# Biases on diagonals minus weights: a set-up step moved to GpSimd, and a new order of the beginning and the end

## The chip, the cores and the metric

The kernel runs on one core of a Trainium2 chip. The metric is the device time of one execution in microseconds (us). A core has five engines with their own instruction queues: TensorE (PE; its weight loads are shown as PEld), VectorE (DVE), ScalarE (ACT), GpSimd (POOL) and SyncE (SP), which here only issues transfers. They meet through semaphores: an instruction waits for a count, and later instructions of the same queue wait behind it.

## The reference

The input x has 32 sequences of 256 tokens with 128 channels. The reference is one layer of a transformer, cut here to what is computed:

```
n  = layernorm(x)                                  # over the 128 channels
Q, K, V = n W_Q + b_Q, n W_K + b_K, n W_V + b_V    # 16 heads of 64
A  = softmax(Q K^T / 8)
y  = concat(A V) W_O + b_O
x1 = x + layernorm(y)
m  = layernorm(x1)
z  = m W + (1/16) sum_e softmax(m G)_e * V_e U_e m   # 8 experts of rank 16
out = x1 + layernorm(z)
```

All of it is in float32. For every query, key and weight of the attention the kernel keeps a high part and a low part (`_hi`, `_lo`), and it forms the products of high with high, high with low and low with high.

## The kernel before

A sequence is worked on in eight pairs of heads. For each pair TensorE projects queries and keys (`project_qk`, lines 434 to 436, into the bank `qk_ps`). ScalarE takes the high part, VectorE or GpSimd the low part (`qk_lo`). TensorE forms the scores (`scores`, line 468, into one of two banks `st_ps`), VectorE finds the row maxima (`row_max`, line 1317), ScalarE the exponentials (line 860), VectorE the inverse sums and GpSimd scales the probabilities (`scale_probs`, line 1805). VectorE transposes them in blocks (`transpose_blocks`), SyncE moves the blocks of four pairs with 16 transfers (`move_blocks`, line 313), and TensorE multiplies with the values (`probs_v`, line 493). Then come the output projection (line 527), the layer norms and the experts. Several sequences are in flight: the scores of sequence i, the probabilities times values of i - 1 and i - 2, and the rest of i - 3 or i - 4.

The order of the work is written out by hand for each engine: a beginning (sequences 0 to 3), a loop whose body stands once per sequence (4 to 30), and an end (31 and what is left of 28 to 30). The loop is the same before and after the change.

The set-up is done once in the beginning. The layer norm before the projections has a constant of 1 added to every channel instead of the bias (line 841, `xt_high`), so each query and key weight needs a correction: bias minus column mean of the weights. `weight_means` makes it on TensorE in six pieces. The first two pieces are the 256 early columns of the query and of the key weights, the other four are 384 late columns each. For a piece, one product of a matrix of -1/128 with the weights (line 379) gives minus the mean, and for each pair of heads one product of a broadcast bias column with the identity over 128 (line 383) adds the bias. VectorE adds the result to the weights (`fold_means`, line 1223); ScalarE and VectorE then split the weights in a high and a low part (`weight_hi`, line 834, and `weight_lo`, line 1214). `value_sums` (line 392) sums the value weights with 8 products of one column each. GpSimd centres the output weights (`centre_w_o`, line 1763), and VectorE centres the rows of the experts' weights (`centre_ffn_rows`, lines 1283 to 1290).

## Time and profile before

| | |
|---|---|
| time, median of 3 runs (lowest to highest) | 978.57 us (977.16 to 979.06) |
| the profiled execution's own time | 978.71 us |
| its span between first and last instruction | 976.9 us |
| granted TensorE clock, mean over the span | 0.998 of full speed |
| busy: PE / PEld | 963.7 us (99%) / 777.3 us (80%) |
| busy: DVE / ACT / POOL | 909.9 us (93%) / 887.9 us (91%) / 759.9 us (78%) |

The span starts with the first instruction on any engine. The time has 1.8 us more than the span, which lie around it. A matmul in float32 is recorded as two instructions, so a product that stands once in the program can be counted twice in the trace.

### The profile page before, as it was taken

Reading aid. Unit: us, or ns where it says so; the run is one execution under the profiler, and the core shown is the slowest. Engines: PE = TensorE matmul, PEld = TensorE weight load, DVE = VectorE, ACT = ScalarE, POOL = GpSimd, SP = SyncE. Lnnn points to the kernel's source line nnn. Section 1 sums busy time; section 2 is a strip of 40 time slices with the busy share of each in tenths; the row PEclk is TensorE's granted clock in tenths of the full one; section 3 lists DMA queues with packets and bytes.
Section 4 is the critical chain, followed back from the end, with each engine's and each line's share of the span. In section 5 each row is a group of like instructions: output and inputs, shape, how many; then the busy total and the mean of one; then the engine's idle time right before and its main releaser. Section 6 shows DMA issues by size and latency. Waiting matters only on the chain.

```text
span 976.9 us, 28184 instructions
## 1 busy us (share of the span) xinstructions
PE 963.7 (99%) x8628; PEld 777.3 (80%) x8628; DVE 909.9 (93%) x1666; ACT 887.9 (91%) x3183; POOL 759.9 (78%) x746
## 2 busy tenths in 40 slices
PE   8999999999999999999999999999999999999997
PEld 7768888778888878888878888877888877878875
DVE  5999999999999999999999999999999999999972
ACT  4999999999999999999999999999999999999872
POOL 2777988888888788878878878887888878877862
PEclk9999999999999999999999999999999999999999
DMA  7276775666676665676666676566677666667560
GB/s 267 55 164 138 171 164 134 141 151 137 158 172 139 137 153 137 148 177 144 138 151 138 137 177 155 137 149 141 138 166 164 138 138 152 138 156 167 131 157 12
DMA packets 58467, 143.32 MB, mean 147 GB/s; under 512 B 16960, under 2 KB 25664, under 8 KB 58432
## 3 DMA queue, kind: packets, MB, share of 16 engines
q1 hardware_dynamic: 58432, 142.89, 63.4%
q8 instruction: 18, 0.29, 0.1%
q14 instruction: 17, 0.14, 0.0%
HBM read 6.50 MB, written 4.19 MB: 11 GB/s over the span
## 4 chain that ended last, share of the span: by engine, by line
PE 93%; SPq 2%; DVE 2%; ACT 1%; issue 1%; DMA 0%; POOL 0%; POOLq 0%; DVEq 0%; ACTq 0%
PE o_ps L493 24%; PE st_ps L468 21%; PE extra_ps L527 9%; PE qk_ps L434 6%; PE qk_ps L435 6%; PE qk_ps L436 6%; PE xv_ps L448 4%; PE extra_ps L358 3%; PE xv_ps L450 3%; PE xv_ps L449 3%; PE extra_ps L549 2%; SPq L313 2%; PE extra_ps L562 2%; PE extra_ps L564 1%; PE xv_ps L358 1%
## 5 line engine op out<-in xcount | busy, mean ns | idle before, releaser
L1805 POOL TENSOR_TENSOR probs<-probs,inv_sum 128x1024 f32<-128x1024 f32 x256 | 484.4, 1896 | 115.6 <-DVE inv_sum L1325 108.4
L860 ACT ACTIVATE probs<-st_ps,neg_max 128x256 f32<-128x256 f32 x1024 | 476.8, 496 | 33.6 <-DVE neg_max L1317 31.8
L1317 DVE TENSOR_REDUCE neg_max<-st_ps 128x4 f32<-128x1024 f32 x256 | 308.3, 1205 | 12.6 <-PE st_ps L468 11.7
L1336 DVE STREAM_TRANSPOSE probs_b<-probs 128x1024 f32<-128x1024 f32 x252 | 309.0, 1229 | 1.1 <-POOL probs L1805 1.1
L493 PE MATMUL o_ps<-probs_t,v_sb 128*64 128x256 f32 x2048 | 249.3, 385 | 1.6 <-DMA probs_t<-probs_b 0.9
L860 ACT ACTIVATION_READ_ACCUMULATOR probs<-st_ps,neg_max 128x1 f32 x1024 | 231.5, 226 | 0.0
L493 PEld LDWEIGHTS o_ps<-probs_t,v_sb 128*64 128x64 f32 x2048 | 135.9, 136 | 81.1 <-DVE o_lo L1351 10.4
L468 PE MATMUL st_ps<-qk_hi 64*128 64x256 f32 x1024 | 162.8, 314 | 1.3 <-ACT probs L860 0.8
L846 ACT CAST qk_hi<-qk_ps 128x512 fp32r<-128x512 f32 x256 | 153.2, 598 | 11.9 <-PE qk_ps L436 7.0
L468 PE MATMUL st_ps<-qk_lo,qk_hi 64*128 64x256 f32 x1024 | 145.4, 279 | 0.0
L468 PE MATMUL st_ps<-qk_hi,qk_lo 64*128 64x256 f32 x1024 | 144.8, 278 | 0.0
L1312 DVE TENSOR_TENSOR qk_lo<-qk_ps,qk_hi 128x512 fp32r<-128x512 f32 x192 | 130.3, 678 | 6.2 <-ACT qk_hi L846 2.4
L468 PEld LDWEIGHTS st_ps<-qk_hi 64*128 64x128 f32 x1024 | 97.1, 186 | 28.0 <-issue 7.2
L1351 DVE TENSOR_TENSOR o_lo<-o_ps,o_hi 128x512 fp32r<-128x512 f32 x128 | 87.7, 685 | 13.7 <-ACT o_hi L875 10.0
L468 PEld LDWEIGHTS st_ps<-qk_lo,qk_hi 64*128 64x128 f32 x1024 | 98.0, 187 | 0.0
L468 PEld LDWEIGHTS st_ps<-qk_hi,qk_lo 64*128 64x128 f32 x1024 | 98.0, 187 | 0.0
L1778 POOL TENSOR_TENSOR rstd<-var_eps,neg_half 128x2 f32<-128x2 f32 x128 | 88.9, 694 | 10.0
L875 ACT CAST o_hi<-o_ps 128x512 fp32r<-128x512 f32 x128 | 80.2, 627 | 7.1 <-PE o_ps L493 7.0
L434 PE MATMUL qk_ps<-xt_hi,wq_hi 128*128 128x256 f32 x256 | 84.4, 330 | 1.3 <-DVE qk_lo L1312 0.6
L1799 POOL TENSOR_TENSOR qk_lo<-qk_full,qk_hi 128x512 fp32r<-128x512 f32 x64 | 82.2, 1284 | 3.6 <-ACT qk_full L853 2.0
L882 ACT COPY v_sb<-xv_ps 128x512 f32<-128x512 f32 x128 | 77.2, 603 | 0.3 <-PE xv_ps L450 0.3
L527 PE MATMUL extra_ps<-o_hi,wo_hi 128*128 128x256 f32 x256 | 72.6, 284 | 0.0
(140 smaller groups left out, 1952.6 us busy)
## 6 DMA issues: line engine op xcount, KB each, us to landing
probs_t<-probs_b SPq DMA_DIRECT2D x1008, 128.0 KB, 2.3
out<-x_all SPq DMA_DIRECT2D x31, 128.0 KB, 1.9
x_all<-in_x SPq DMA_DIRECT2D x1, 3840.0 KB, 17.4
probs_b<-in_w_v SPq DMA_DIRECT2D x1, 512.0 KB, 4.5
probs_b<-in_w_o SPq DMA_DIRECT2D x1, 512.0 KB, 6.3
probs_b<-in_w_q SPq DMA_DIRECT2D x1, 384.0 KB, 4.8
probs_b<-in_w_k SPq DMA_DIRECT2D x1, 384.0 KB, 5.4
x_all<-in_x SPq DMA_DIRECT2D x2, 128.0 KB, 3.2
```

Source lines behind the costliest of these rows:

```text
L434: nc.tensor.matmul(dst, w_hi[w][:, cols], xt_hi[turn][:, :], start=True, stop=False)
L468: last = nc.tensor.matmul(st_ps[p % 2][:, (2 * h + j) * T:(2 * h + j + 1) * T], tile(q, j)[head_rows(h), :], k[head_rows(h), :], start=(t ...
L493: last = nc.tensor.matmul(o_ps[head_rows(h), cols], v_sb[turn][:, s, p * P + h * DH:p * P + (h + 1) * DH], probs_t[chunk % 2][:, :, s, fir ...
L527: last = nc.tensor.matmul(extra_ps[:, 0:T], w["o"][:, cols], o[:, pair, :], start=(pair == pairs[0] and n == 0), stop=(pair == pairs[-1] a ...
L846: nc.scalar.copy(qk_hi_sb[p % N_QK][:, :], qk_ps[:, :]).then_inc(qk_hi_ready, 1)
L860: last = nc.scalar.activation(probs[n][:, h, j, :], st_ps[p % 2][:, (2 * h + j) * T:(2 * h + j + 1) * T], ACT.Exp, bias=neg_max[n][:, h, j ...
L1312: nc.vector.tensor_tensor(qk_lo_sb[n][:, :], qk_ps[:, :], f32(qk_hi_sb[n][:, :]), ALU.subtract).then_inc(qk_lo_ready, 1)
L1317: nc.vector.tensor_reduce(neg_max[p % N_PROBS][:, :, :].rearrange("p h j -> p (h j)"), st_ps[p % 2][:, :].rearrange("p (j s) -> p j s", j= ...
L1336: nc.vector.transpose(probs_b[chunk % 2][:, :, :, 2 * NT * n:2 * NT * (n + 1), :].rearrange("p i t n q -> p n t i q"), probs[p % N_PROBS][ ...
L1351: nc.vector.tensor_tensor(o_lo[:, pairs, :].rearrange("p g q -> p (g q)"), o_ps[:, :], f32(o_hi[:, pairs, :]).rearrange("p g q -> p (g q)" ...
L1778: nc.gpsimd.tensor_tensor(rstd[ln][:, :], var_eps[ln][:, :], neg_half[:, :], ALU.pow).then_inc(rstd_ready[ln], 1)
L1805: nc.gpsimd.tensor_tensor(probs[n][:, :, :, :].rearrange("p h j s -> p (h j) s"), probs[n][:, :, :, :].rearrange("p h j s -> p (h j) s"), ...
```

## The change

For the four late pieces the two kinds of products become one. GpSimd makes, for queries and for keys, a tensor of 128 by 768 (`less`): it puts the biases on the diagonals of six 128 by 128 blocks (`bias_on_diagonal`) and, when the late weights have landed, subtracts them (`less_weights`). The column mean of that tensor is bias over 128 minus the mean weight on every row, which one product with a matrix of 1/128 gives (`mean_w`). The two early pieces stay as they were. The tensors `less` lie in the buffer into which the first blocks of probabilities are moved later, so the first `move_blocks` waits for the sixth piece.

The hand-written order of the beginning and of the end changes on all engines. The core of the diff, with the functions in full and of the orders the places that matter below:

```diff
+        less = {n: probs_t[0][:, i, :, :, :].rearrange("p t n q -> p (t n q)")[:, 0:(PAIRS - 2) * P] for i, n in enumerate("qk")}
...
             def move_blocks(b, chunk):
                 transposed = PAIRS * b + (chunk + 1) * CHUNK
+                if first(b) and chunk == 0:
+                    sp.wait_ge(mean_projected, len(MEANS))
...
             def weight_means(piece):
 
                 n, cols, bank = MEANS[piece]
...
+                else:
+                    if piece >= 3:
+                        pe.wait_ge(mean_folded, piece)
+                    pe.wait_ge(less_ready[n], 1)
+                    last = nc.tensor.matmul(bank[:, 0:cols.stop - cols.start], mean_w[:, :],
+                                            less[n][:, cols.start - 2 * P:cols.stop - 2 * P], start=True, stop=True)
                 last.then_inc(mean_projected, 1)
...
             weight_means(1)
+            value_sums()
+            weight_means(2)
             transpose_xn(0)
-            weight_means(2)
+            weight_means(3)
             project_qk(0, 0, 0)
-            weight_means(3)
+            weight_means(4)
             project_v(0, 0, 0, free=(xt_lo_ready, 1))
-            weight_means(4)
+            weight_means(5)
             project_qk(0, 1, 0)
-            weight_means(5)
             scores(0, 0)
-            value_sums()
+            project_v(0, 1, 0, free=(v_copied[0], 1))
             project_qk(0, 2, 0)
...
+            store(29)
             move_blocks(31, 0)
-            store(29)
...
+            def bias_on_diagonal(n):
+
+                pool.wait_ge(bias_loaded, 16)
+                pool.wait_ge(constants_ready, 1)
+                column = (B_Q if n == "q" else B_K) + 2
+                nc.gpsimd.tensor_tensor(per_pair(less[n]), ident[:, :].unsqueeze(1).to_broadcast([P, PAIRS - 2, P]),
+                                        bias[:, column:column + PAIRS - 2].unsqueeze(2).to_broadcast([P, PAIRS - 2, P]),
+                                        ALU.mult).then_inc(diagonal_ready[n], 1)
+
+            def less_weights(n):
+                pool.wait_ge(diagonal_ready[n], 1)
+                pool.wait_ge(w_loaded[n], 16)
+                nc.gpsimd.tensor_tensor(less[n], less[n], stage[n][:, late],
+                                        ALU.subtract).then_inc(less_ready[n], 1)
...
+            bias_on_diagonal("q")
+            bias_on_diagonal("k")
             ln_rstd(LN_X, 1)
-            centre_w_o()
+            less_weights("q")
+            less_weights("k")
             ln_rstd(LN_X, 2)
             qk_lo(0, 1)
+            centre_w_o()
             scale_probs(0, 0)
```

In the queue of GpSimd the beginning of the set-up stood like this before (`probs_b` is where the loaded weights are staged, `var_eps` and `rstd` belong to the layer norms, `qk_lo` to the first pair that GpSimd splits):

```order
L1828 AFFINE_SELECT ident<-ident 128x128
L1771 TENSOR_TENSOR var_eps<-mean_var,eps 128x2
L1778 TENSOR_TENSOR rstd<-var_eps,neg_half 128x2
L1763 TENSOR_TENSOR probs_b<-probs_b,w_o_mean 128x1024
L1771 TENSOR_TENSOR var_eps<-mean_var,eps 128x2
L1778 TENSOR_TENSOR rstd<-var_eps,neg_half 128x2
L1799 TENSOR_TENSOR qk_lo<-qk_full,qk_hi 128x512
L1805 TENSOR_TENSOR probs<-probs,inv_sum 128x1024
```

The same place on GpSimd now (`probs_t` is the buffer in which `less` lies):

```order
L1854 AFFINE_SELECT ident<-ident 128x128
L1784 TENSOR_TENSOR probs_t<-ident,bias 128x768 x2
L1797 TENSOR_TENSOR var_eps<-mean_var,eps 128x2
L1804 TENSOR_TENSOR rstd<-var_eps,neg_half 128x2
L1791 TENSOR_TENSOR probs_t<-probs_t,probs_b 128x768 x2
L1797 TENSOR_TENSOR var_eps<-mean_var,eps 128x2
L1804 TENSOR_TENSOR rstd<-var_eps,neg_half 128x2
L1825 TENSOR_TENSOR qk_lo<-qk_full,qk_hi 128x512
L1771 TENSOR_TENSOR probs_b<-probs_b,w_o_mean 128x1024
L1831 TENSOR_TENSOR probs<-probs,inv_sum 128x1024
```

Four operations of 768 columns are new, two of them behind the first `rstd`, and the centring of the output weights has gone behind the first `qk_lo`.

In the queue of VectorE the set-up went on after the two early folds like this before (`xt_lo` is the low part of the transposed input, `wv_lo` and the like are low parts of weights, folds are the additions of `o_ps`):

```order
L1214 SCALAR_TENSOR_TENSOR wq_lo<-probs_b,wq_hi 128x256
L1214 SCALAR_TENSOR_TENSOR wk_lo<-probs_b,wk_hi 128x256
L1266 SCALAR_TENSOR_TENSOR xt_lo<-xv_ps,xt_hi 128x256
L1223 TENSOR_TENSOR probs_b<-probs_b,o_ps 128x384
L1214 SCALAR_TENSOR_TENSOR wv_lo<-probs_b,wv_hi 128x1024
L1312 TENSOR_TENSOR qk_lo<-qk_ps,qk_hi 128x512
L1223 TENSOR_TENSOR probs_b<-probs_b,o_ps 128x384
L1272 TENSOR_REDUCE w_o_mean<-probs_b 128x8
L1275 TENSOR_SCALAR w_o_mean<-w_o_mean 128x8
L1223 TENSOR_TENSOR probs_b<-probs_b,o_ps 128x384
L1283 TENSOR_REDUCE ffn_mean<-ffn 128x1 x2
L1286 TENSOR_SCALAR ffn_mean<-ffn_mean 128x2
```

The same place on VectorE now, from the normalisation of the first x on:

```order
L1258 TENSOR_SCALAR xn<-x_all,mean_var,rstd 128x128 x2
L1233 TENSOR_TENSOR probs_b<-probs_b,st_ps 128x256
L1224 SCALAR_TENSOR_TENSOR wv_lo<-probs_b,wv_hi 128x1024
L1224 SCALAR_TENSOR_TENSOR wk_lo<-probs_b,wk_hi 128x256
L1250 BN_AGGR mean_var<-stats 128x2 x2
L1233 TENSOR_TENSOR probs_b<-probs_b,o_ps 128x384
L1224 SCALAR_TENSOR_TENSOR wq_lo<-probs_b,wq_hi 128x256
L1276 SCALAR_TENSOR_TENSOR xt_lo<-xv_ps,xt_hi 128x256
L1233 TENSOR_TENSOR probs_b<-probs_b,o_ps 128x384
L1282 TENSOR_REDUCE w_o_mean<-probs_b 128x8
L1285 TENSOR_SCALAR w_o_mean<-w_o_mean 128x8
L1233 TENSOR_TENSOR probs_b<-probs_b,o_ps 128x384
```

The low part of the value weights and the first late fold now stand ahead of `xt_lo`, for which the first projection waits, and the rows of the experts' weights are no longer centred here.

They are centred on VectorE during the scores of sequence 1, where these rows stand now:

```order
L1322 TENSOR_TENSOR qk_lo<-qk_ps,qk_hi 128x512
L1293 TENSOR_REDUCE ffn_mean<-ffn 128x1 x2
L1296 TENSOR_SCALAR ffn_mean<-ffn_mean 128x2
L1300 TENSOR_SCALAR ffn<-ffn,ffn_mean 128x128 x2
L1335 RECIPROCAL inv_sum<-row_sum 128x4
```

Nothing of the experts stood between the low parts and the inverse sums of that place before.

## Rows read from the trace of the kernel before

**Rows 1.** Windows: start:end, us, busy us of each engine, clock, DMA share, GB/s

```profile
core 0: us, PE busy (x) PEld busy (x) DVE busy (x) ACT busy (x) POOL busy (x), PEclk, DMA share, GB/s
30.00:40.00 10.00, 9.87 (x84) 8.22 (x84) 9.68 (x18) 9.41 (x32) 8.35 (x8) 1.00 0.01 3
40.00:50.00 10.00, 8.55 (x74) 6.61 (x72) 9.82 (x15) 10.00 (x38) 9.26 (x7) 1.00 0.70 157
60.00:70.00 10.00, 10.00 (x88) 7.15 (x89) 9.31 (x15) 8.55 (x28) 6.53 (x7) 1.00 0.62 141
950.00:960.00 10.00, 8.59 (x71) 5.72 (x69) 4.15 (x14) 4.26 (x16) 2.37 (x6) 1.00 0.23 55
```

**Rows 2.** Timeline of TensorE in the set-up: start, us, engine, line, what [idle before]

```profile
11.05 0.36 PE L434 MATMUL qk_ps<-xt_hi,wq_hi 128*128 128x256 f32 x1 [0.34 <-DVE xt_lo L1266]
...
12.49 0.83 PE L383 MATMUL o_ps<-probs_t,bias 128*128 128x128 f32 x6
13.07 0.48 PE L448 MATMUL xv_ps<-wv_hi,xt_hi 128*128 128x512 f32 x1
...
18.61 1.95 PE L392 MATMUL st_ps<-one,probs_b 128*128 128x1 f32 x16
20.41 0.36 PE L434 MATMUL qk_ps<-xt_hi,wq_hi 128*128 128x256 f32 x1
```

**Rows 3.** Timeline of SyncE's queue: the issue of the late query weights

```profile
3.54 0.43 SPq L297 DMA_DIRECT2D probs_b<-in_w_q  x1
```

**Rows 4.** DMA issues: KB each, us from issue to landing

```profile
probs_b<-in_w_q SPq DMA_DIRECT2D x1, 384.0 KB, 4.8
```

**Rows 5.** Timeline of GpSimd in the set-up

```profile
15.32 1.90 POOL L1763 TENSOR_TENSOR probs_b<-probs_b,w_o_mean 128x1024 f32<-128x1024 f32 x1 [10.46 <-DVE w_o_mean L1275]
...
19.79 1.58 POOL L1799 TENSOR_TENSOR qk_lo<-qk_full,qk_hi 128x512 fp32r<-128x512 f32 x1 [1.64 <-ACT qk_hi L846]
27.59 1.89 POOL L1805 TENSOR_TENSOR probs<-probs,inv_sum 128x1024 f32<-128x1024 f32 x1 [6.22 <-DVE inv_sum L1325]
```

**Rows 6.** Line 1799 over the whole span: ns min/median/max, first and last start

```profile
L1799 POOL TENSOR_TENSOR qk_lo<-qk_full,qk_hi x64: 1272/1279/1579, 19.8 to 926.8; 128x512 fp32r<-128x512 f32 x64
```

**Rows 7.** Timeline of VectorE in the set-up

```profile
15.07 0.17 DVE L1275 TENSOR_SCALAR w_o_mean<-w_o_mean 128x8 f32<-128x8 f32 x1
...
16.05 0.47 DVE L1283 TENSOR_REDUCE ffn_mean<-ffn 128x1 f32<-128x128 f32 x2
16.56 0.69 DVE L1286 TENSOR_SCALAR ffn_mean<-ffn_mean 128x2 f32<-128x2 f32 x1
17.28 0.48 DVE L1290 TENSOR_SCALAR ffn<-ffn,ffn_mean 128x128 f32<-128x128 f32 x2
...
19.27 0.96 DVE L1214 SCALAR_TENSOR_TENSOR wk_lo<-probs_b,wk_hi 128x768 fp32r<-128x768 f32 x1
20.15 1.22 DVE L1317 TENSOR_REDUCE neg_max<-st_ps 128x4 f32<-128x1024 f32 x1
...
22.22 0.69 DVE L1312 TENSOR_TENSOR qk_lo<-qk_ps,qk_hi 128x512 fp32r<-128x512 f32 x1 [0.78 <-ACT qk_hi L846]
24.47 1.23 DVE L1317 TENSOR_REDUCE neg_max<-st_ps 128x4 f32<-128x1024 f32 x1 [1.55 <-PE st_ps L468]
25.61 1.22 DVE L1214 SCALAR_TENSOR_TENSOR wo_lo<-probs_b,wo_hi 128x1024 fp32r<-128x1024 f32 x1
```

**Rows 8.** Windows, as rows 1, behind the value sums

```profile
23.00:24.00 1.00, 1.00 (x10) 1.00 (x12) 0.00 (x0) 1.00 (x7) 0.00 (x0) 0.50 0.00 0
```

**Rows 9.** Timeline of the end, TensorE, GpSimd and SyncE

```profile
935.01 1.95 PE L493 MATMUL o_ps<-probs_t,v_sb 128*64 128x256 f32 x16 [0.91 <-DMA probs_t<-probs_b]
...
959.90 0.38 PE L527 MATMUL extra_ps<-o_hi,wo_hi 128*128 128x256 f32 x1
...
943.27 0.75 POOL L1816 TENSOR_TENSOR x_all<-z,x 128x256 f32<-128x256 f32 x1
...
940.69 10.10 SPq L313 DMA_DIRECT2D probs_t<-probs_b  x16
```

More of the change, by code:

```diff
@@ L327, in _ @@
             move_blocks(2, 1)
+            move_blocks(3, 0)
             store(0)
-            move_blocks(3, 0)
             move_blocks(3, 1)
@@ L615, in _ @@
             project_qk(1, 0, 1)
-            project_v(1, 1, 1, free=(v_copied[0], 2))
             scores(0, 6)
@@ L647, in _ @@
             project_qk(2, 2, 0)
+            project_v(2, 1, 0, free=(v_copied[0], 3))
             ffn_means()
@@ L653, in _ @@
             project_qk(2, 3, 0)
-            project_v(2, 2, 0, free=(v_copied[1], 3))
             output_projection(0)
@@ L670, in _ @@
             scores(2, 5)
+            transpose_xn(3, free=(v_copied[3], 3))
             project_qk(2, 7, 0)
-            project_v(3, 0, 1, free=(xt_lo_ready, 4))
             scores(2, 6)
             project_tg(0, free=(x1t_ready, 1))
+            project_v(3, 0, 1, free=(xt_lo_ready, 4))
             project_qk(3, 0, 1)
+            scores(2, 7)
             project_v(3, 1, 1, free=(v_copied[0], 4))
+            project_qk(3, 1, 1)
             probs_v(1, 4, 1)
             probs_v(1, 5, 1)
-            project_qk(3, 1, 1)
-            scores(2, 7)
             scores(3, 0)
@@ L685, in _ @@
             probs_v(1, 7, 1)
+            scores(3, 1)
             project_z(0, free=(ut_ready, 1))
@@ L688, in _ @@
             project_v(3, 2, 1, free=(v_copied[1], 4))
-            scores(3, 1)
             scores(3, 2)
+            project_v(3, 3, 1, free=(v_copied[2], 4))
             project_qk(3, 4, 1)
-            project_v(3, 3, 1, free=(v_copied[2], 4))
             output_projection(1, free=(z_copied, 1))
@@ L940, in _ @@
             weight_hi("v", every, w_hi_ready)
+            weight_hi("k", early, early_hi_ready, 2)
             weight_hi("q", early, early_hi_ready, 1)
-            weight_hi("k", early, early_hi_ready, 2)
             xt_high(0, 0)
+            weight_hi("q", late, w_hi_ready, 4)
             qk_hi(0, 0)
-            weight_hi("q", late, w_hi_ready, 4)
             copy_v(0, 0, 0)
-            qk_full(0, 1)
-            weight_hi("o", every, w_hi_ready)
             weight_hi("k", late, w_hi_ready, 6)
             qk_hi(0, 1)
+            qk_full(0, 1)
+            copy_v(0, 1, 0)
             qk_hi(0, 2)
+            exponentials(0, 0, 1)
             exponentials(0, 0, 0)
-            exponentials(0, 0, 1)
-            copy_v(0, 1, 0)
+            copy_v(0, 2, 0)
             qk_hi(0, 3)
+            exponentials(0, 1, 0)
             exponentials(0, 1, 1)
-            exponentials(0, 1, 0)
-            copy_v(0, 2, 0)
             qk_hi(0, 4)
+            exponentials(0, 2, 1)
             exponentials(0, 2, 0)
-            exponentials(0, 2, 1)
             copy_v(0, 3, 0)
@@ L965, in _ @@
             exponentials(0, 3, 0)
+            xt_high(1, 1)
             qk_hi(0, 6)
             exponentials(0, 3, 1)
-            xt_high(1, 1)
-            exponentials(0, 4, 1)
+            weight_hi("o", every, w_hi_ready)
             qk_hi(0, 7)
             exponentials(0, 4, 0)
+            exponentials(0, 4, 1)
             copy_v(1, 0, 1)
@@ L1183, in _ @@
-            copy_last(4)
             exponentials(31, 7, 1)
@@ L1414, in _ @@
             spread_x(1)
+            fold_means(0)
             norm_first_x()
+            fold_means(1)
+            weight_lo("v", every, w_hi_ready, w_lo_ready)
             spread_landed(LN_X, 1)
-            settle()
+            weight_lo("k", early, early_hi_ready, early_lo_ready)
             aggregate_x(1)
-            fold_means(0)
-            fold_means(1)
+            fold_means(2)
             weight_lo("q", early, early_hi_ready, early_lo_ready)
-            weight_lo("k", early, early_hi_ready, early_lo_ready)
             xt_low(0, 0)
-            fold_means(2)
-            weight_lo("v", every, w_hi_ready, w_lo_ready)
-            qk_lo(0, 0)
             fold_means(3)
@@ L1429, in _ @@
             fold_means(4)
-            centre_ffn_rows()
+            qk_lo(0, 0)
+            offset_values()
             fold_means(5)
@@ L1842, in _ @@
             scale_probs(0, 4)
+            qk_lo(1, 1)
             scale_probs(0, 5)
-            norm_x(2)
-            qk_lo(1, 1)
             scale_probs(0, 6)
@@ L1927, in _ @@
             ln_rstd(LN_Y, 30)
+            ln_rstd(LN_X1, 30)
+            qk_lo(31, 5)
             scale_probs(31, 1)
-            qk_lo(31, 5)
-            ln_rstd(LN_X1, 30)
             scale_probs(31, 2)
```

531 lines of the change are left out of this document (267 added, 264 removed).

## The prediction

> **What bounds the kernel now.** I read the windows first, to see which stretches leave TensorE idle. From 60 to 70 us TensorE is busy without a gap [rows 1], and so it stays through the loop, which the change leaves alone: there TensorE is the bound. The beginning is different. Between 30 and 50 us VectorE is busy 9.68 and 9.82 of 10 us and ScalarE 9.41 and 10.00, while TensorE misses 1.45 us of the second ten [rows 1]. Until about 55 us the chain through row maxima and exponentials sets the pace, and a microsecond counts there only if VectorE's list gets shorter or starts earlier. The end has gaps again, 1.41 us from 950 to 960 [rows 1]. Then I read the timelines of the set-up, to see who waits for whom, and that of the end. A gain in the beginning reaches the end whole if it still stands when TensorE becomes the bound.
>
> **The four products.** A late piece's six recorded bias products stand from 12.49 to 13.07 us, 0.58 us [rows 2]. Four pieces free 4 x 0.58 = 2.3 us of TensorE. In the loop that would be 2.3 us of the time. Here TensorE runs ahead of VectorE, so I cost it at nothing by itself; the second rival below lives on it.
>
> **The value sums.** They take 18.61 to 20.41, 1.80 us [rows 2], and move ahead of the third piece. There TensorE will wait for VectorE anyway (below), which hides them. At the old place they leave room, but VectorE's weight work lasts to 20.15 [rows 7], so their going gains at most 0.26 us by itself.
>
> **The new work on GpSimd.** The trace has no such operation of 768 columns. From below it is bounded by 1.28 us for 512 [rows 6], from above by 1.90 us for 1024 [rows 5]. I take 1.5 us for each diagonal and, as two full tensors are read, 1.8 us for each subtraction. The diagonals lie in an empty stretch: GpSimd idles 10.46 us before 15.32 [rows 5]. The first `rstd` is queued behind them and comes about 3 us later; the normalisation that waits for it now stands behind a fold on VectorE, so that this is hidden too. The subtraction for q starts when the late query weights have landed, at 3.54 + 4.8 = 8.34 us [rows 3, 4], and the one for k would end at about 12.0 if nothing interfered. TensorE's third piece waits for the first of them, and behind it in TensorE's queue stand the transposes of the first x and every projection. The first `move_blocks` waits for the sixth piece, which is made long before the first blocks are; it costs nothing.
>
> **What interferes.** Two places show VectorE and GpSimd holding each other up. GpSimd's low part takes 1.272 to 1.279 us at the least and in the median of 64 cases, but 1.579 in one [rows 6]: the first, at 19.79, while VectorE's `wk_lo` of 19.27, which reads two tensors from SBUF, still ran [rows 5, 7]. The 0.30 us are about what was left of that operation. The other way round, the scaling of `ffn_mean` (2 columns) took 0.69 us where its sister of 8 columns took 0.17 [rows 7]: it started at 16.56 and ended at 17.25, when GpSimd's centring of 15.32 had ended at 17.22 [rows 5]. So a VectorE operation with two inputs in SBUF, or a scaling from SBUF to SBUF, does not run beside a GpSimd operation that reads SBUF. After the change such pairs meet: from 8.34 to about 12 us VectorE wants to normalise the first x and to make `wv_lo` and `wk_lo`.
>
> The Trainium skill ("SBUF — State Buffer", section "Who interferes with whom") has this as a rule that speaks against the change: the two engines share one pair of ports, held for a whole instruction, by a VectorE operation with two SBUF inputs or in a two-port mode. By that rule the new work costs waits on both engines; without it the sum would be that of the first rival. The trace agrees in the two places just named.
>
> So I lay the work end to end: 8.34, two subtractions (3.6), `wv_lo` (1.2, as `wo_lo`), `wk_lo` and `wq_lo` of the early columns (at most 0.45 each, as 768 columns take 0.96) [rows 7], one fold (0.5, a 384-wide operation, by half of the same row), and `xt_lo` with an aggregation (0.5, an estimate from the same row). That is 15.0. If VectorE gets some turns between the subtractions it is 14.3, if it loses all of them 15.8. The first projection, at 11.05 now [rows 2], then starts at 15.0.
>
> From there to the first row maximum VectorE has three more folds (1.5), the means of the output weights (1.2, a reduction as wide as a row maximum's 1.22, and 0.17), a `qk_lo` (0.6), the value offset (0.15) and the two late low parts (1.9) [rows 7]: 5.5 us. The row maximum stands at 20.5 against 20.15 now: **+0.35**.
>
> **After the first row maximum.** Now VectorE waits 0.78 and then 1.55 us [rows 7]. The second wait is for scores that TensorE made late and slowly: the granted clock was 0.50 from 23 to 24 [rows 8], the lower level of 1.2 GHz, after the value sums, which moved single columns. With the value sums done early the two waits may go: 0 to -2.3, and I take **-2.3**, since the second quarter of the values is projected ahead of time as well. The centring of the experts' rows comes into this full stretch: 0.47 + 0.69 + 0.48 = 1.64 as it stood, 1.12 without its own wait [rows 7]; between them **+1.4**. The low part `wo_lo` moves from 25.61, where GpSimd was in 6.22 us of idle time [rows 5, 7], to a place beside scalings of 1.89 us [rows 5]: it waits 0 to 1.9. Since the next inverse sum stands behind it on VectorE, at most one scaling runs then; I take **+0.5**. The beginning: 0.35 - 2.33 + 1.4 + 0.5 = -0.1 us.
>
> **The end.** The work is the same in another order. TensorE waits 0.91 us at 935.01 for blocks of sequence 30 [rows 9]. VectorE's new order finishes the last of these transposes some 1.2 us earlier (a row maximum of 1.22 us [rows 7] moves behind it), but TensorE comes earlier too, since project_qk(31, 7) and scores(31, 6) now stand behind. I walked on with the durations of before and find the last output projection 0.5 us earlier than 959.90 [rows 9]: **-0.5**. The bounds are -2.3, if the 0.91 and 1.41 us of gaps close, and +1.5, if as much opens. What follows it is unchanged. On SyncE store(29) stands ahead of the last sixteen transfers; GpSimd has its data one scaling earlier than now, so I cost it at nothing (the last rival is its price).
>
> **Sum.** -0.1 - 0.5 = -0.6 us on the profiled execution's own 978.71 us gives 978.1; that execution lies 0.14 above the median, so 978.0 against 978.57. About 0.2% (2.0 us) is what a measurement of this kernel can tell from no change. The forecast is no change that can be told, with an own range of 976.6 to 979.8.
>
> **Rivals.**
> *No mutual wait (chance 0.27).* If the normalisation and the low parts run beside the subtractions, the first projection needs q's subtraction (10.15), one product (0.7), a fold, `wq_lo` and `xt_lo` (1.5) and some 0.7 of hand-overs: 13.0 instead of 15.0, and `wo_lo` costs nothing. That is 2.5 us better than the forecast: 975.5. For it: in the loop the two engines run side by side all the time. Against it: the rows of 1.58 and 0.69 us.
> *All of TensorE's saving arrives (0.05).* The 2.3 us of products and VectorE's 2.3 us of waits both come off: 974.0. Against it: 9.82 of 10 us on VectorE.
> *Slower: GpSimd wins every turn (0.18).* It takes k's subtraction directly behind q's, and later a scaling ahead of `wo_lo`. The first projection starts at 15.8 (0.8 more); TensorE stands idle for some 3 us right behind the value sums, its clock falls as before 23 us, and a piece's products take twice their 0.58 (0.6 more); `wo_lo` waits all its 1.9 (1.4 more). That is 2.8 us worse: 980.8. It decides from a first projection behind 15.8.
> *Slower: the store holds the last blocks (0.05).* The sixteen transfers start at 940.69 now, and the data of store(29) was ready at 943.27 + 0.75 = 944.0 [rows 9]. If it comes no earlier, they start up to 3.3 us later; half of that as the price gives 979.7.
> The forecast has 0.45. Faster by over 0.2% are the first two, 0.32; slower the last two, 0.23. The range of 975.2 to 980.6 reaches into both sides and leaves out their far ends, about 0.2 together.
>
> **What would show it.** In the profile after: two GpSimd operations of about 1.8 us from 8.3 us on; the normalisation of x, `wv_lo` or `wk_lo` lasting far longer than its width explains; the first projection near 15.0 and the first row maximum near 20.5 us; a long `wo_lo`; the last output projection 0.6 us earlier than 959.9. A first projection near 13 us beside short low parts would prove the first rival. TensorE idle between 60 and 70 us, where it has no gap now, would break the whole sum.

## The result and the profile after

The changed kernel takes 982.63 us in the median of 8 runs (980.67 to 985.34), the kernel before 978.62 in 8 runs beside it. The ratio is 1.0043, with its 95% interval in brackets [1.0032, 1.0054]: 4.0 us slower by the medians, and above the range of the prediction (975.2 to 980.6). The profiled execution took 983.44 us, 0.8 above the median, with a span of 981.66 against 976.92.

Three landmarks split the 4.74 us between the two spans: the first row maximum on VectorE, the 16th output projection on TensorE (in the unchanged loop), and the end of the span.

| | first projection | first row maximum | from there to the 16th output projection | from there to the end |
|---|---|---|---|---|
| before | 11.05 | 20.15 | 493.34 | 463.43 |
| after | 15.19 | 23.11 | 494.01 | 464.54 |
| difference | +4.14 | +2.96 | +0.67 | +1.11 |

So most of the loss is made before the first row maximum. The windows of the changed kernel (start, length, busy us of each engine, granted clock, DMA share, GB/s), the last four of which answer to [rows 1]:

```profile
10.00:20.00 10.00, 7.31 (x23) 5.11 (x23) 8.01 (x13) 2.00 (x5) 4.55 (x4) 0.67 1.07 381
30.00:40.00 10.00, 9.57 (x77) 8.16 (x75) 9.85 (x15) 9.39 (x32) 8.17 (x7) 0.87 0.01 2
40.00:50.00 10.00, 8.84 (x73) 7.12 (x73) 9.14 (x13) 9.03 (x31) 7.16 (x4) 0.96 0.61 136
60.00:70.00 10.00, 9.78 (x89) 6.95 (x85) 10.00 (x17) 8.98 (x32) 5.48 (x5) 1.00 0.57 128
950.00:960.00 10.00, 8.50 (x70) 6.01 (x72) 5.66 (x21) 4.50 (x17) 3.80 (x6) 1.00 0.60 136
```

The first line is the one to look at: from 10 to 20 us TensorE is busy 7.31 of 10 us, and its granted clock is 0.67 in the mean, so it ran for a large part at the lower level of 1.2 GHz. GpSimd's timeline (start, duration, instruction, in brackets the idle time before it) shows the new work, where [rows 5] had nothing:

```profile
3.14 2.89 POOL L1784 TENSOR_TENSOR probs_t<-ident,bias 128x768 f32<-128x768 f32 x2 [0.89 <-DMA bias<-in_biases]
8.73 4.66 POOL L1791 TENSOR_TENSOR probs_t<-probs_t,probs_b 128x768 f32<-128x768 f32 x2 [1.75 <-DMA probs_b<-in_w_q]
23.30 1.29 POOL L1825 TENSOR_TENSOR qk_lo<-qk_full,qk_hi 128x512 fp32r<-128x512 f32 x1 [8.15 <-ACT qk_full L863]
```

The two subtractions (L1791) fill 8.73 to 13.39 us. VectorE beside them, and on to the first row maximum [rows 7]:

```profile
8.89 0.41 DVE L1233 TENSOR_TENSOR probs_b<-probs_b,st_ps 128x256 f32<-128x256 f32 x1
9.22 2.50 DVE L1224 SCALAR_TENSOR_TENSOR wv_lo<-probs_b,wv_hi 128x1024 fp32r<-128x1024 f32 x1
11.65 2.02 DVE L1224 SCALAR_TENSOR_TENSOR wk_lo<-probs_b,wk_hi 128x256 fp32r<-128x256 f32 x1
...
13.75 0.52 DVE L1233 TENSOR_TENSOR probs_b<-probs_b,o_ps 128x384 f32<-128x384 f32 x1
...
16.00 0.56 DVE L1233 TENSOR_TENSOR probs_b<-probs_b,o_ps 128x384 f32<-128x384 f32 x1 [1.07 <-PE o_ps L394]
...
18.57 0.56 DVE L1233 TENSOR_TENSOR probs_b<-probs_b,o_ps 128x384 f32<-128x384 f32 x1 [0.67 <-PE o_ps L394]
...
20.77 0.55 DVE L1233 TENSOR_TENSOR probs_b<-probs_b,o_ps 128x384 f32<-128x384 f32 x1 [0.98 <-PE o_ps L394]
...
23.11 1.22 DVE L1327 TENSOR_REDUCE neg_max<-st_ps 128x4 f32<-128x1024 f32 x1
```

Two things are to be seen. The low parts are stretched: `wv_lo` lasts 2.50 us where `wo_lo`, as wide, took 1.22 [rows 7], and a `wk_lo` of 256 columns lasts 2.02 us, more than one of 768 columns (0.96 in [rows 7]). Because of the two the third fold comes at 13.75, though its weight mean was done at 11.6. Then each later fold waits for TensorE, 1.07 + 0.67 + 0.98 = 2.72 us. And TensorE [rows 2]:

```profile
8.65 1.84 PE L402 MATMUL st_ps<-one,probs_b 128*128 128x1 f32 x16
10.70 0.91 PE L394 MATMUL o_ps<-probs_t,mean_w 128*128 128x384 f32 x2 [0.20 <-POOL probs_t L1791]
11.45 0.38 PE L363 MATMUL xv_ps<-ident,xn 128*128 128x128 f32 x2
14.32 1.65 PE L394 MATMUL o_ps<-probs_t,mean_w 128*128 128x384 f32 x2 [2.49 <-DVE probs_b L1233]
15.19 0.99 PE L444 MATMUL qk_ps<-xt_hi,wq_hi 128*128 128x256 f32 x1
```

It stood idle for 2.49 us until the third fold was done. A weight mean (L394) of the same size took 0.91 us ahead of the gap and 1.65 behind it; the granted clock is 0.50 from 13.4 to 20.2 us, as windows of 1 us show:

```profile
12.00:13.00 1.00, 0.00 (x0) 0.00 (x0) 1.00 (x1) 0.34 (x1) 1.00 (x1) 1.00 1.09 387
14.00:15.00 1.00, 0.68 (x1) 0.50 (x2) 0.93 (x3) 0.00 (x0) 0.92 (x2) 0.50 1.09 387
19.00:20.00 1.00, 1.00 (x3) 0.75 (x3) 0.79 (x3) 0.15 (x1) 0.00 (x0) 0.50 1.09 389
21.00:22.00 1.00, 1.00 (x14) 0.86 (x14) 1.00 (x2) 0.64 (x1) 0.00 (x0) 1.00 0.03 11
```

At the end the chain of waits (start, us, what) runs through SyncE's queue [rows 9]:

```profile
929.14 0.59 SPq L318
929.77 1.72 SPq L318
931.53 0.59 SPq L318
...
935.34 2.48 DMA probs_t<-probs_b
937.87 1.95 PE o_ps L503 x16
```

SyncE issues one transfer behind the other here, each in 0.59 us; one took 1.72, and TensorE waited 1.16 us for the last of them:

```profile
937.87 0.87 PE L503 MATMUL o_ps<-probs_t,v_sb 128*64 128x256 f32 x6 [1.16 <-DMA probs_t<-probs_b]
```

### The profile page after: what moved, and what is told of

Its sections match the earlier page's. It is cut to its first block, busy times and chain, and to the rows that moved or that the text cites. A ratio compares the mean times of both kernels' runs of the same rounds, so it can differ in the third digit from the quotient of the medians.

```text
span 981.7 us, 28141 instructions
## 1 busy us (share of the span) xinstructions
PE 963.9 (98%) x8604; PEld 776.4 (79%) x8604; DVE 912.6 (93%) x1664; ACT 887.8 (90%) x3183; POOL 767.0 (78%) x750
## 4 chain that ended last, share of the span: by engine, by line
PE 90%; DVE 3%; SPq 2%; ACT 2%; issue 1%; DMA 1%; POOL 0%; POOLq 0%; DVEq 0%; ACTq 0%
PE o_ps L503 23%; PE st_ps L478 20%; PE extra_ps L537 9%; PE qk_ps L444 6%; PE qk_ps L446 6%; PE qk_ps L445 6%; PE xv_ps L458 4%; PE extra_ps L363 3%; PE xv_ps L460 3%; PE xv_ps L459 3%; SPq L318 2%; PE extra_ps L559 2%; PE extra_ps L572 2%; PE extra_ps L574 1%; ACT probs L870 1%
## 5 line engine op out<-in xcount | busy, mean ns | idle before, releaser
L1327 DVE TENSOR_REDUCE neg_max<-st_ps 128x4 f32<-128x1024 f32 x256 | 307.9, 1204 | 12.8 <-PE st_ps L478 11.6
L870 ACT ACTIVATION_READ_ACCUMULATOR probs<-st_ps,neg_max 128x1 f32 x1024 | 228.5, 223 | 0.0
L1361 DVE TENSOR_TENSOR o_lo<-o_ps,o_hi 128x512 fp32r<-128x512 f32 x128 | 87.7, 685 | 13.4 <-ACT o_hi L885 10.0
L444 PE MATMUL qk_ps<-xt_hi,wk_hi 128*128 128x256 f32 x256 | 72.6, 284 | 0.0
```

Source lines behind the costliest of these rows:

```text
L444: nc.tensor.matmul(dst, w_hi[w][:, cols], xt_hi[turn][:, :], start=True, stop=False)
L870: last = nc.scalar.activation(probs[n][:, h, j, :], st_ps[p % 2][:, (2 * h + j) * T:(2 * h + j + 1) * T], ACT.Exp, bias=neg_max[n][:, h, j ...
L1327: nc.vector.tensor_reduce(neg_max[p % N_PROBS][:, :, :].rearrange("p h j -> p (h j)"), st_ps[p % 2][:, :].rearrange("p (j s) -> p j s", j= ...
L1361: nc.vector.tensor_tensor(o_lo[:, pairs, :].rearrange("p g q -> p (g q)"), o_ps[:, :], f32(o_hi[:, pairs, :]).rearrange("p g q -> p (g q)" ...
```

## The experiments

Each experiment was timed beside the kernel before, whose medians there were 978.46 to 978.82 us; each ratio is taken to it. The interval of a ratio is 0.9 to 1.7 us to either side, so a difference between the medians of two experiments is uncertain by 1.3 us or more. The landmarks come from one profiled execution of each kernel. In the expectations a remainder is a low part.

**First split: end, beginning, products, clock.** Experiment 1 has only the new end:

```diff
             store(28)
+            store(29)
             move_blocks(31, 0)
-            store(29)
```

and the same for the other engines' lists behind the loop.

> The kernel before with the new order of the last blocks alone (all five engines from block 30 on). In the two traces the steady stretch of the changed kernel lies 3.65 us later and its end 1.08 us later again. Theory A (two separate losses, the set-up 3.65 and the end 1.1): 978.6 + 1.1 = 979.7 us, first output projection at 74.7 as before, last one at 961.0. Rival B (the end is neutral and lost its microsecond only because it was entered in another state): 978.6 us within 0.3.

Measured: 978.88 us, ratio 1.000 [0.9991, 1.0010]. By itself the new end neither costs nor gives anything that can be told; theory A's sum of two separate losses fails here, and rival B holds. Experiment 2 is the rest of the change without those hunks.

> The changed kernel with the old order of the last blocks: GpSimd's work and the new order of the beginning alone. Theory A: 978.6 + 3.65 = 982.2 us, TensorE idle 2.5 us before the fourth weight mean, granted clock near 0.67 between 10 and 20 us, first output projection at 77.6, last one at 963.5. Rival B: the whole loss sits here, 982.6 us or more, and the old end gives nothing back.

Measured: 980.87 us, ratio 1.0029 [1.0019, 1.0039]. That is below both expectations. Half of the loss or more sits in the beginning, and the new beginning is 1.8 us better by the medians with the old end than with the new one; the two intervals still overlap. Its profiled execution met the weights' landing 1 us later, `wv_lo` escaped (1.22 us), `wk_lo` did not (2.02). Experiment 3 keeps the new orders and takes GpSimd's work away:

```diff
-            bias_on_diagonal("q")
-            bias_on_diagonal("k")
-            less_weights("q")
-            less_weights("k")
```

with `weight_means` of the kernel before.

> The changed kernel in its new orders, but the four late weight means are made as before (one mean product and three bias products each, straight from the loaded weights), and GpSimd makes no diagonals and subtracts nothing. Theory A (VectorE and GpSimd hold each other up, TensorE stands idle behind them and its clock falls): wv_lo and the early wk_lo back to 1.22 and 0.42 us, no idle of 2.5 us, no clock fall between 13 and 20 us, first row max at 20 to 20.5 in place of 23.1, first output projection at 74 to 75.5, and 979 to 980 us, the rest being the end's 1.1. Rival C (the new order itself is at fault: value sums and the value remainder put ahead of the folds): first row max still at 22 or later and 981.5 us or more.

Measured: 980.45 us, 1.0015 [1.0005, 1.0024], between the two theories. VectorE's remainders are short again and the clock is 1.00 from 10 to 20 us, yet the first projection stands at 14.80 and the first row maximum at 21.88 (this execution, of 981.55 us, was the slowest of the 11):

```profile
9.55 1.84 PE L397 MATMUL st_ps<-one,probs_b 128*128 128x1 f32 x16
11.25 0.89 PE L384 MATMUL o_ps<-probs_b,probs_t 128*128 128x384 f32 x2
...
13.46 0.91 PE L384 MATMUL o_ps<-probs_b,probs_t 128*128 128x384 f32 x2 [0.43 <-DVE probs_b L1228]
14.21 0.83 PE L388 MATMUL o_ps<-probs_t,bias 128*128 128x128 f32 x6
14.80 0.37 PE L439 MATMUL qk_ps<-xt_hi,wq_hi 128*128 128x256 f32 x1
```

VectorE's folds wait for TensorE here:

```profile
12.85 0.56 DVE L1228 TENSOR_TENSOR probs_b<-probs_b,o_ps 128x384 f32<-128x384 f32 x1 [1.05 <-PE o_ps L388]
15.08 0.56 DVE L1228 TENSOR_TENSOR probs_b<-probs_b,o_ps 128x384 f32<-128x384 f32 x1 [1.00 <-PE o_ps L388]
...
17.31 0.56 DVE L1228 TENSOR_TENSOR probs_b<-probs_b,o_ps 128x384 f32<-128x384 f32 x1 [0.34 <-PE o_ps L388]
...
19.54 0.55 DVE L1228 TENSOR_TENSOR probs_b<-probs_b,o_ps 128x384 f32<-128x384 f32 x1 [1.00 <-PE o_ps L388]
...
21.88 1.22 DVE L1322 TENSOR_REDUCE neg_max<-st_ps 128x4 f32<-128x1024 f32 x1
```

So the new order with the old products is slower than before as well: value sums and two whole weight means stand ahead of the first projection, and TensorE is the chain. Experiment 4 was to hold the clock:

```diff
             transpose_xn(0)
+            warm_up(5)
             weight_means(3)
```

> The changed kernel with five more throw-away products (0.46 us each, as in its warm-up) behind the first transposes, where TensorE stood idle 2.5 us. VectorE's and GpSimd's work is untouched. Theory A1 (the fall of the clock after that idle costs most of the loss at the first row max): clock 1.0 through 10 to 20 us, the fourth weight mean 0.9 us long in place of 1.65, VectorE's three waits for folds down from 2.7 to below 1 us in sum, first row max at 21.0 to 21.5, and 980.5 us. Rival A2 (VectorE's lengthened remainders are the loss, the clock is hidden behind them): row max at 22.5 or later and 982 to 983 us.

Measured: 981.67 us, 1.0034 [1.0022, 1.0046]. It did not test what it should: in this execution TensorE stood idle 2.29 us already ahead of the third weight mean, the clock was 0.83 from 10 to 20 us, and the throw-away products ran behind that gap.

**Second split: order, products, and what VectorE is held up by.** Experiment 5 is the kernel before with the new products alone: the four calls above on GpSimd, `weight_means` of the changed kernel, all old orders.

> The kernel before in all its old orders, with the new products alone: GpSimd makes the diagonals and subtracts the weights (ahead of its old work on w_o), and the four late weight means are one product each. With the new order and old products it took 1.6 us more than before, with both 3.8 more. Theory A (order and GpSimd's subtractions each cost about half): VectorE's early remainders are stretched as in the changed kernel, first row max at 21 to 22, 980 to 981 us. Rival D (the new products cost something only in the new order, where the first projection stands behind two of them): first projection at 11 to 12, first row max at 20 or earlier, 978 to 979 us.

Measured: 981.53 us (978.51 to 983.94 in 12 runs), 1.0027 [1.0013, 1.0040]. Nearer to theory A and above its range; rival D falls, with the first projection at 12.78 and the first row maximum at 22.74. The wide spread goes with the core's mean granted clock: the three executions with 1.0 took 978.5 to 979.4 us, the five with 0.992 to 0.994 took 982.6 to 983.9. The profiled one has 0.993: `wk_lo` at 2.02 us, TensorE idle 2.85 us ahead of the third weight mean, clock 0.83 and 0.66 in the second and third ten us. Experiment 6:

```diff
             weight_means(1)
-            value_sums()
             weight_means(2)
...
             scores(0, 0)
+            value_sums()
```

and on VectorE the use of the sums (`offset_values`) behind the first row maximum.

> The changed kernel with the value sums (16 products, 1.84 us) and VectorE's use of them put back behind the first scores. Theory A (TensorE waits for GpSimd's first subtraction there anyway, which ends at about 11 us, while the sums end at 10.5): first projection still at 15 and no gain, 982 to 983 us, perhaps 0.5 more since the sums now stand in a busy stretch. Rival E (the sums ahead of the third weight mean are what delays the first projection): first projection at 13.4, first row max at 21.3, 980.8 us.

Measured: 983.90 us, 1.0061 [1.0047, 1.0074]; first projection 15.58, first row maximum 23.13. Theory A, with 0.4 us more than it allowed: with the subtractions in the way the new place of the sums is free. That the old place costs more is not shown, since the row maximum stands as in the changed kernel and the two intervals overlap. Experiment 7:

```diff
-            weight_lo("v", every, w_hi_ready, w_lo_ready)
             spread_landed(LN_X, 1)
...
             fold_means(3)
+            weight_lo("v", every, w_hi_ready, w_lo_ready)
```

> The changed kernel with one VectorE instruction moved: the remainder of the value weights (wv_lo) behind the fourth fold in place of ahead of the third, so that it no longer lies beside GpSimd's subtractions. Theory A (VectorE, held up in wv_lo and wk_lo by GpSimd, comes late to the third fold, and TensorE waits for that): the fold at 12 in place of 13.75, first projection at 13 to 13.7, first row max at 21 to 21.7, 980.5 to 981.3 us. Rival F (the chain of weight means and folds through the one bank decides, whatever VectorE does beside it): first row max still at 22.5 or later, 982 us or more.

Measured: 980.96 us, 1.0033 [1.0021, 1.0045]. First projection 13.85, first row maximum 21.27: theory A, with the first projection 0.15 us later than it said. One VectorE instruction moved out of GpSimd's way gives 1.84 us at the first row maximum, and 1.7 of the 4.0 by the medians. Experiment 8 takes away what stands in the way:

```diff
-                nc.gpsimd.tensor_tensor(less[n], less[n], stage[n][:, late],
+                nc.gpsimd.tensor_tensor(less[n][:, 0:1], less[n][:, 0:1], stage[n][:, 256:257],
```

> The changed kernel, but GpSimd subtracts only one column of each late weight block (so the late means of query and key weights are wrong); diagonals, products and orders are kept. Theory A (the two subtractions, 4.6 us of GpSimd, hold up VectorE and TensorE): no stretched remainders, third weight mean at 10.5 right behind the value sums, first projection at 12.5 to 13.5, first row max at 20 to 20.8, 979 to 979.8 us. Rival C (the new order is what costs): 980.4 us or more, as with the old products.

Measured: 978.64 us, 1.0007 [0.9998, 1.0016]: no difference from the kernel before that can be told. The loss is gone, more of it than expected. TensorE's line of the set-up:

```profile
8.70 1.84 PE L402 MATMUL st_ps<-one,probs_b 128*128 128x1 f32 x16
10.41 0.89 PE L394 MATMUL o_ps<-probs_t,mean_w 128*128 128x384 f32 x2
11.14 0.38 PE L363 MATMUL xv_ps<-ident,xn 128*128 128x128 f32 x2
11.95 0.91 PE L394 MATMUL o_ps<-probs_t,mean_w 128*128 128x384 f32 x2 [0.43 <-DVE probs_b L1233]
12.71 0.36 PE L444 MATMUL qk_ps<-xt_hi,wq_hi 128*128 128x256 f32 x1
```

and VectorE's first row maximum:

```profile
18.59 1.22 DVE L1327 TENSOR_REDUCE neg_max<-st_ps 128x4 f32<-128x1024 f32 x1
```

No gap over 0.43 us, clock 1.00, and the first row maximum at 18.59, 1.56 us ahead of the kernel before. Up to this landmark orders and products are a gain as long as the subtraction takes no time; with the new end the gain does not reach the time.

**Third split: clock, held-up VectorE, or late data; and the end.** Experiment 9 fills both gaps:

```diff
             value_sums()
+            warm_up(3)
             weight_means(2)
             transpose_xn(0)
+            warm_up(5)
             weight_means(3)
```

> The changed kernel with throw-away products in both places where TensorE waited for GpSimd: three ahead of the third weight mean (1.4 us) and five behind the first transposes. In the fourth experiment TensorE had stood idle ahead of the third mean and the clock fell all the same, so that run did not test the clock. Theory A1 (the fall of the clock costs about half of the 4 us): granted clock 1.0 from 10 to 20 us, first row max at 21 to 21.7, 980.3 to 981 us. Rival A2 (only waiting and the stretched remainders count): clock 1.0, row max still at 22.3 or later, 982 us or more.

Measured: 980.40 us, 1.0022 [1.0013, 1.0031]. The window from 10 to 20 us, with the clock at 1.00, and VectorE's timeline:

```profile
10.00:20.00 10.00, 8.97 (x57) 6.55 (x59) 9.29 (x18) 3.46 (x7) 3.27 (x4) 1.00 1.07 381
```

```profile
8.69 3.50 DVE L1260 TENSOR_SCALAR xn<-x_all,mean_var,rstd 128x128 f32<-128x128 f32 x2
12.11 0.41 DVE L1235 TENSOR_TENSOR probs_b<-probs_b,st_ps 128x256 f32<-128x256 f32 x1
12.44 1.21 DVE L1226 SCALAR_TENSOR_TENSOR wv_lo<-probs_b,wv_hi 128x1024 fp32r<-128x1024 f32 x1
...
21.29 1.22 DVE L1329 TENSOR_REDUCE neg_max<-st_ps 128x4 f32<-128x1024 f32 x1
```

```profile
15.40 0.36 PE L444 MATMUL qk_ps<-xt_hi,wq_hi 128*128 128x256 f32 x1
```

VectorE was held up as much as in the changed kernel (2.9 us, as there 1.28 in `wv_lo` and 1.60 in `wk_lo`), this time in the normalisation, which takes 0.60 us by itself, so that the first projection is at 15.40, no earlier than in the changed kernel. Yet the row maximum is at 21.29: TensorE's products behind the gap run at full clock. Theory A1: at the first row maximum the clock alone is worth 1.82 us. The medians differ by 2.2, but there the end plays in: in the two profiled executions it is 0.8 us shorter here (463.75 against 464.54 us from the 16th output projection). Experiment 10 lets GpSimd work beside VectorE while nobody waits for the result. TensorE's products wait for the diagonals and the landed weights and leave the weights' means out; of the diff this is the subtraction alone:

```diff
-                nc.gpsimd.tensor_tensor(less[n], less[n], stage[n][:, late],
+                nc.gpsimd.tensor_tensor(spare[n], less[n], stage["v"][:, late],
```

> The changed kernel, but GpSimd's two subtractions write a spare buffer and read the value weights, and the four late weight means go on with the diagonals alone as soon as the weights have landed (so the weights' own means are left out). GpSimd works beside VectorE as long as before; nobody waits for its result. Theory A3 (the stretched VectorE instructions are the loss): wv_lo and wk_lo at 2 to 2.5 us, third fold at 13.5, first projection at 15, row max at 22 to 23, 981.5 us or more. Rival G (the loss is the waiting for the subtracted weights, 4.6 us for two): third mean at 10.3, first row max at 19 to 20, 979 to 979.8 us, with the remainders stretched all the same.

Measured: 982.23 us (978.67 to 983.99 in 8 runs), 1.0039 [1.0021, 1.0056]; first projection 15.76, first row maximum 22.67. Theory A3: the loss does not need the wait for GpSimd's data, VectorE standing still brings it, with the fall of the clock behind it (0.83 from 10 to 20 us). What was caught is the normalisation, not the low parts as expected. VectorE and GpSimd side by side in this kernel:

```profile
8.99 3.45 DVE L1262 TENSOR_SCALAR xn<-x_all,mean_var,rstd 128x128 f32<-128x128 f32 x2
```

```profile
8.79 3.56 POOL L1796 TENSOR_TENSOR probs_t<-probs_t,probs_b 128x768 f32<-128x768 f32 x2 [1.87 <-DMA probs_b<-in_w_k]
```

One begins 0.2 us behind the other, and they end within 0.1 us. Experiment 11 is the eighth with the old end (the hunk of experiment 1 undone).

> The eighth experiment (one column subtracted by GpSimd) with the old order of the last blocks. The traces from the 16th output projection to the end: 463.4 to 463.7 us with the old end in three kernels, 464.4 to 464.9 with the new end in five of seven, where one transfer issue of SP took 1.7 to 2.1 us in place of 0.6 just ahead of the products that wait for it. Theory H (the new end has no slack for such a long issue and pays 1.1 us where it falls there): 977.5 us, stretch from the 16th output projection at 463.4 to 463.7. Rival B (the end is neutral, as it was alone): 978.6 us.

Measured: 977.41 us, 0.9996 [0.9986, 1.0005], stretch from the 16th output projection 463.68. Theory H by its numbers, but not by its reason: this kernel has two long issues as well, and TensorE waits 1.14 us for the transfers, against 1.24 in experiment 8. What the old end saves of this stretch (463.68 against 464.65 us) lies elsewhere, as told below. The kernel leaves out almost the whole subtraction, so it is no kernel to use; it bounds what the beginning could give. Experiment 12 tries to keep the change:

```diff
+            def subtract_q():
+                nc.vector.tensor_tensor(less["q"], less["q"], stage["q"][:, late], ALU.subtract)
...
-            less_weights("q")
             less_weights("k")
```

with `wv_lo` moved as in experiment 7 and the old end.

> A version meant to keep the change and lose the waits: VectorE subtracts the query weights itself (768 columns, about 0.95 us as its remainder of the same size) ahead of the first remainders, GpSimd only the key weights, the value remainder stands behind the fourth fold as in the seventh experiment, and the last blocks keep their old order. Theory A: third mean at 10.5 with no idle, clock 1.0 through 10 to 20 us, first row max at 19.5 to 20.3, 977.5 to 978.6 us. Rival (VectorE is the chain here and any microsecond put on it shows): row max at 21, 979.5 us.

Measured: 979.83 us, 1.0015 [1.0006, 1.0024]; third mean at 10.88 and clock 1.00, but `wk_lo` still 2.03 us beside the one subtraction left, and the row maximum at 21.04. The rival, by 0.3 us more than it said.

**What was left open.** Experiment 13 adds to the first one the single wait that the changed kernel has on SyncE:

```diff
+                if first(b) and chunk == 0:
+                    sp.wait_ge(mean_projected, len(MEANS))
```

> The first experiment (old beginning, new end, 978.9 us) with one SP wait more, the one that the changed kernel has ahead of its first probability transfers and that nothing waits for. It makes SP's program one instruction longer, as in all kernels whose new end cost 1.2 us. Theory J (SP's long transfer issues fall on fixed places of its program, and the added instruction moves one onto the transfers that the new end waits for): 979.7 to 980.1 us, a long issue among the 36th to 39th from the last, stretch from the 16th output projection at 464.4 or more. Rival K (the place of the long issue has nothing to do with that wait): 978.9 us, stretch at 463.5.

Measured: 978.92 us, 1.0003 [0.9994, 1.0013], stretch 463.45. Theory J falls. Experiment 14 joins experiments 7 and 9 with the old end (`warm_up(3)` and `warm_up(1)`, `wv_lo` later).

> The change with what the experiments gave: value remainder behind the fourth fold, three throw-away products ahead of the third weight mean and one behind the first transposes, old order of the last blocks. By sums: 980.96 of the seventh experiment, less 1.2 for the old end, less about 1 for a clock that stays at 1.0 through 10 to 20 us: 978.6 to 979 us, first row max at 20.2 to 20.6. Rival (the stretched remainders alone still cost about 1.8 us, as between the eighth and the ninth experiment): 979.2 to 980 us, row max at 21.

Measured: 980.38 us, 1.0018 [1.0009, 1.0026]; row maximum 21.06. The rival, 0.4 us above its range: with the clock at 1.00 from 10 to 20 us and VectorE's low parts short but for `wk_lo` (0.99 us), the third weight mean still came at 11.82 behind the throw-away products and the first projection at 14.04. No version that computes everything beats the kernel before.

## Why the prediction was wrong

**The step that failed** is the one from the first projection to the first row maximum, "5.5 us" of VectorE work. Up to it the reasoning held: mutual waits were forecast, the first projection was put at 15.0 with them and 13.0 without, and it stood at 15.19, and at 12.60 and 12.71 when only one column was subtracted (experiments 11 and 8). That the 15.0 came so close is in part luck: VectorE had `wv_lo` between the two subtractions, a turn for which the forecast said 14.3, but the subtractions began at 8.73, not at 8.34, and the weight mean ahead of the projection ran at the lower clock. From there the step counted VectorE's list as if TensorE kept ahead at full clock. The distance from the first projection to the row maximum was 5.88 us in experiments 8 and 11 and 5.89 in experiment 9, all with the clock at 1.00: the term was nearly right for that. In the changed kernel it was 7.92, since the idle time that the mutual waits make lies right in front of it, the clock fell to 0.50, and each of three folds waited for a slow weight mean. That is 2.0 us, and experiment 9, which held the clock, has its row maximum 1.82 us earlier.

The fall was in the text, but in the rival in which GpSimd wins every turn, as something that begins at a first projection behind 15.8. That point was wrong: 15.19 was late enough, because TensorE was already idle for 2.49 us. A forecast of 15.0 held the same gap, and the clock belonged into its sum. With these 2.0 us it would have said 980.0, still 2.6 too low. Over the three stretches of the table the forecast was +0.35, -0.4 and -0.5, the measurement +2.96, +0.67 and +1.11; so of 5.3 us missed in the spans 2.6 lie ahead of the first row maximum, 1.1 behind it and 1.6 in the end.

The other steps:

- *The four products at nothing.* Wrong for the new order. There experiment 3 (old products) has its row maximum at 21.88 and experiment 8 (short products, almost no subtraction) at 18.59; 0.85 us of this is a later start (value sums at 9.55 against 8.70). In experiment 3 VectorE's four folds waited 3.39 us for TensorE, in experiment 8 0.67: TensorE's chain of weight means and folds through one bank was the limit, which the prediction gave to VectorE. The medians differ by 1.8 us, but the intervals of the ratios overlap. For the old order no run tests it; in the kernel before VectorE waited 0.34 us for these products.
- *The value sums.* Hidden, as said (experiment 6).
- *GpSimd's durations.* 1.47 us for a diagonal (1.5 taken). A subtraction took 1.80 us where VectorE stood still for it (1.8 taken), 1.92 and 2.78 in the changed kernel, and up to 2.86 where it had to wait itself (experiment 4). The reading of 0.30 us as what was left of `wk_lo` at 19.79 was rough: by [rows 5, 7] 0.44 us were left.
- *The mutual waits.* Right in kind, and shown by experiment 10. Between experiments 9 and 8, both at full clock up to the first row maximum, they take 2.70 us there beside the clock's 1.82; by the medians 1.8, with the uncertainty above.
- *After the first row maximum.* Forecast -2.3 + 1.4 + 0.5 = -0.4, measured +0.67. The row maxima's waits for scores went, from 2.4 to 0.3 us in the first 110 us. But the experts' rows took 1.75 us, `wo_lo` 2.03 in place of 1.22, and with a second fall of the clock, from 37.3 to 40.7 us, came a new wait of 0.86 on VectorE. Of the twelve profiled kernels with the new order of the beginning, the six whose clock fell between 34.7 and 40.7 us show such a wait there (the longest of each 0.34 to 0.94 us), the six others none; why the clock fell there no run shows:

```profile
41.75 0.69 DVE L1322 TENSOR_TENSOR qk_lo<-qk_ps,qk_hi 128x512 fp32r<-128x512 f32 x1 [0.86 <-ACT qk_hi L856]
...
43.55 2.03 DVE L1224 SCALAR_TENSOR_TENSOR wo_lo<-probs_b,wo_hi 128x1024 fp32r<-128x1024 f32 x1
```

- *The end.* Forecast -0.5, measured +1.1; the last output projection, forecast 0.6 us earlier than 959.90, came at 964.62. The blocks of sequence 30 were not earlier, as the step had it from VectorE's order: SyncE's queue, one issue per 0.63 us, sets when they land. The rival of the store did not decide: its transfers follow at 944.66, and in experiment 11, with the old order of stores, at 939.91, against 939.97 in experiment 8 with the new one.

The end in numbers: over ten kernels with the new end, the stretch from the 16th output projection is 463.3 to 463.5 us plus what TensorE waits for these transfers (0 us: 463.45; 0.42: 463.75; 1.16: 464.54; 1.53: 464.89). Over six with the old end it is 462.5 to 462.6 plus the wait (0.91: 463.43; 1.38: 463.88). So the new end is about 0.9 us longer in itself. With the old beginning it met no wait and came out even; with the new one it met 0.4 to 1.5. In the kernels with the new end that wait went with the number of long issues of SyncE between 911 and 935 us: none or 0.4 us of wait with one, 0.7 us and more with two. Why there are two in six of the eight kernels that have both the new beginning and the new end is open; a further instruction on SyncE does not bring them (experiment 13). What makes the new end longer in itself is open too.

## What to carry to other kernels

Where one engine's idle time grows in a forecast, ask at once what TensorE's clock does behind that gap, and count the next few microseconds of its products at the lower level (6.8 us here). The slow stretch behind the gap cost 1.8 us here, in addition to the gap. Work moved to GpSimd is not free because GpSimd is idle: look at what VectorE does in the same microseconds, and count every instruction with two inputs in SBUF, or a scaling from SBUF to SBUF, as standing behind GpSimd's, as they did here. When two engines alternate through one bank, lay both chains out; the one that was bound before the change need not be the one after.

## What the runs showed of the hardware

GpSimd and VectorE held each other up for whole instructions, not in shares. In experiment 9 the two scalings of the normalisation, 0.34 us each otherwise, took 1.74 and 1.84 us, beside subtractions of 1.81 and 1.80: each ended just behind the subtraction that had begun before it. `wk_lo`, 0.42 us by itself, took 2.02 or 2.03 in five kernels. In experiment 4 it was GpSimd that waited: both remainders were short, and the first subtraction took 2.86 us. Which instruction was caught changed with the moment at which the weights landed: with the subtraction begun at 8.54 it was the normalisation (experiment 9), at 8.73 `wv_lo` (the changed kernel). The Trainium skill ("SBUF — State Buffer", section "Who interferes with whom") says that whoever issues first gets the shared ports for the whole instruction and the other is blocked. The trace agrees, with the numbers just given.

Long issues on SyncE were not expected: most take 0.59 us, but single ones 1.0 to 2.2, at changing places of one and the same list.

Ahead of the first projection the clock fell where TensorE had stood idle in one piece for 1.62 us (experiment 2) to 2.85 us (experiment 5), as in the changed kernel and experiments 4, 6 and 10. Where the longest gap was 1.16 us it fell (experiment 7), where it was 1.27 us it did not (experiment 12), nor where it was 0.84 (experiment 9) or 0.43 us (experiments 3, 8 and 11). In the kernel before it fell at 21.0 us with no such gap: TensorE is shown busy throughout from 12 to 21 us, the value sums of single columns among the last of it. The Trainium skill ("TensorE: Matmul & The Clock Gate", section "Part 1: The HAM clock gate") describes the lower level as the state at rest, which activity releases. The trace agrees: throw-away products alone brought the stretch from 10 to 20 us from 0.67 to 1.00 in experiment 9. The fall at 21.0 us in the kernel before is not explained by idle time.
